# Sixteen-head attention: the step for the next operands moved in front of the weighing by key in VectorE's order

## The reference

```python
qkv = (x @ w_qkv.T + b_qkv).reshape(B, T, 3, H, dh)
std_logits = jnp.einsum('bhqd,bhkd->bhqk', q, k) * scale
write_lines = exterior(w1, w2)      # six numbers for each head and position, from x and the position before
read_lines = exterior(r1, r2)
incidence = jnp.einsum('bqhp,bkhp->bhqk', read_lines, J_write)
weights = decays[:, None, None] ** diffs_pos[None] * past[None]
bias = incidence * weights[None] * bias_scale[None, :, None, None]
logits = jnp.where(causal_mask, -jnp.inf, std_logits + bias)
attn = jax.nn.softmax(logits, axis=-1)
out = jnp.einsum('bhqk,bhkd->bqhd', attn, v).reshape(B, T, D)
return out @ w_out.T + b_out
```

## Time and profile before

| | |
|---|---|
| median of 3 runs | 1036.51 us (1032.13 to 1037.96) |
| the profiled execution | 1033.47 us, its span 1032.2 us |
| busy PE, DVE, ACT, POOL | 856.5, 742.6, 655.6, 405.4 us |
| TensorE's granted clock, mean | 0.944 of full |
| the loop over heads | from 328 us to about 838 us; one batch of slots takes 61.5 us |
| chain that ended last | PE 44%, DVE 11%, issue 5%, ACT 5% |

### The profile page before, as it was taken

The page is one execution under the profiler, slowest core; times in us unless marked ns, Lnnn a source line. Parts: engine busy times, 40 slices in busy tenths (PEclk is TensorE's granted clock), DMA queues, the critical chain, the costliest instruction groups (busy, mean ns, idle before and its releaser), DMA issues.

```text
span 1032.2 us, 25478 instructions
## 1 busy us (share of the span) xinstructions
PE 856.5 (83%) x9999; PEld 530.8 (51%) x9999; DVE 742.6 (72%) x1783; ACT 655.6 (64%) x1154; POOL 405.4 (39%) x664
## 2 busy tenths in 40 slices
PE   5688788876565698998989899898888868898987
PEld 2344455554433465665656566575565533444434
DVE  4776888898665868777686877868777557666554
ACT  4668888746234275766667575666656747685866
POOL 3043555455866535373543645454132210101000
PEclk8899999998866599999999999999999989999999
DMA  5000000000324252443525334262542000000000
GB/s 149 22 0 1 1 1 0 1 1 1 105 62 121 68 152 69 116 128 80 148 63 140 86 97 122 68 178 47 143 133 66 3 1 1 22 2 21 1 22 21
DMA packets 70698, 63.60 MB, mean 62 GB/s; under 512 B 30600, under 2 KB 62824, under 8 KB 70576
## 3 DMA queue, kind: packets, MB, share of 16 engines
q1 hardware_dynamic: 70064, 61.90, 22.7%
q10 hardware_dynamic: 512, 0.02, 0.0%
HBM read 34.02 MB, written 27.36 MB: 59 GB/s over the span
## 4 chain that ended last, share of the span: by engine, by line
PE 44%; DVE 11%; issue 5%; ACT 5%; POOL 1%; SPq 1%; DMA 1%; DVEq 0%; POOLq 0%; ACTq 0%
PE bank L2082 12%; PE bank L1660 7%; PE bank L1635 3%; PE bank L1608 3%; PE bank L1616 3%; PE bank L1597 2%; PE bank L1590 2%; DVE bank L1744 2%; PE bank L1600 2%; ACT 4g L2140 1%; PE bank L1668 1%; PE bank L1626 1%; DVE 4f L2176 1%; PE bank L1623 1%; DVE roots L1299 1%
## 5 line engine op out<-in xcount | busy, mean ns | idle before, releaser
L1824 ACT ACTIVATE ET<-bank 64x512 f32<-64x512 f32 x128 | 75.3, 589 | 100.3 <-PE bank L1626 99.5
L2163 DVE TENSOR_TENSOR act<-4f,act 128x512 f16<-128x512 f32 x96 | 66.4, 691 | 56.1 <-ACT act L2130 55.9
L1819 ACT ACTIVATE ET<-bank 128x768 f32<-128x768 f32 x128 | 103.1, 805 | 2.4
L1744 DVE TENSOR_TENSOR bank<-bank,W 128x256 f32<-128x256 f32 x128 | 54.7, 427 | 52.6 <-PE bank L1590 52.6
L1660 PE MATMUL bank<-ET,vv 128*32 128x128 f32 (+2 forms) x1792 | 90.0, 326 | 0.8 <-DVE O L1779 0.8
L1754 DVE TENSOR_REDUCE mo<-bank 128x4 f32<-128x512 f32 x128 | 87.3, 682 | 1.6 <-PE bank L1600 1.4
L1749 DVE TENSOR_TENSOR bank<-bank,WT 128x256 f32<-128x256 f32 x128 | 55.1, 430 | 46.1 <-PE bank L1616 43.2
L2130 ACT ACTIVATE act<-4f 128x512 f16<-128x512 f32 x96 | 60.4, 630 | 28.3 <-DVE 4f L2176 26.2
L1762 DVE TENSOR_REDUCE mo<-bank 128x3 f32<-128x384 f32 x128 | 70.0, 547 | 0.0
L1763 DVE TENSOR_REDUCE mo<-bank 128x3 f32<-128x384 f32 x128 | 69.9, 546 | 0.0
L2082 PE MATMUL bank<-act,std 128*128 128x512 f16 x256 | 57.0, 383 | 0.1
(11 more groups left out here) (376 smaller groups left out, 2542.1 us busy)
## 6 DMA issues: line engine op xcount, KB each, us to landing
ring<-scr_q SPq DMA_DIRECT2D x16, 324.0 KB
QO<-scr_q SPq DMA_DIRECT2D x16, 324.0 KB
ring<-scr_a SPq DMA_DIRECT2D x16, 252.0 KB
KA<-scr_a SPq DMA_DIRECT2D x16, 252.0 KB
ring<-scr_k SPq DMA_DIRECT2D x16, 168.0 KB
KB<-scr_k SPq DMA_DIRECT2D x16, 168.0 KB
scr_a<-dk SPq DMA_DIRECT2D x8, 288.0 KB, 2.6
X<-in_x SPq DMA_DIRECT2D x8, 256.0 KB, 5.2
```

Of the source, the lines that this page charges most:

```text
L1744: dve.tensor_tensor(half(psD, 1), half(psD, 1), over(W[:, h * HB:(h + 1) * HB], NT), ALU.mult).then_inc(s_wq, 1)
L1819: act.activation(ET[n % NE][:, T:SEG * P], psXT[:, 0:NP * P], ACT.Exp).then_inc(s_expo, 1)
L1824: act.activation(to[0:HB, :], psDT[0:HB, :], ACT.Exp)
L2163: dve.tensor_tensor(lo, f32_[f % 3], hi, ALU.subtract).then_inc(s_lo, 1)
```

## The change

One line moves in DVE's loop: `side(n)` goes from the end of the slot, behind `normalise` and `residual`, to between `largest_on_diagonal(n)` and `weigh_by_key(j)`. PE's, ACT's, POOL's and SP's orders stay as they are, and so does every instruction and every wait.

```diff
                 if n < HEADS:
                     largest_on_diagonal(n)
+                side(n)
                 if 0 <= j < HEADS:
                     weigh_by_key(j)
                 q = group_at(n, 4)
@@
                 b = rows_at(n, 1)
                 if b is not None:
                     residual(b)
-                side(n)
                 behind.dve(n)
```

## The result

| | before | after |
|---|---|---|
| median of runs, us | 1036.8 (1032.1 to 1039.2) | 1052.9 (1052.1 to 1057.5), 6 runs |
| ratio to before | | 1.0173, 95% interval [1.0143, 1.0202] |
| the profiled execution: time, span, us | 1033.5, 1032.2 | 1052.5, 1051.2 |
| its mean granted clock | 0.944 | 0.928 |

The kernel became slower by 16.1 us between the medians; the two profiled spans differ by 19.0. By the starts of L1744, 1.3 of these 19.0 lie in front of the loop, 1.3 in its slots 0 to 15, 14.3 in slots 16 to 111 and 2.1 behind them. The forecast was 1049, with 1041 to 1056 as the range.

The account below looks back on a forecast made before the run. PE was taken as nearly the bound, its standing still setting the time. 1033.47 + 10.6 for the order + 2.1 for three clock falls gave 1046.2, or 1049 on the median's level; range 1041 to 1056.

Parts of the forecast that it names:

- slot 2: Second slot of a batch: filling DVE's 0.43 us wait does not pay for 0.57, so PE's L1597 shifts by +0.14 us.
- slot 5: Slot where DVE's step waits for ACT's `raw`: L1749 now starts only when the step ends, L1597 +0.91 us.
- slot 6: Slot with a step 1.48 us long: L1597 at 473.42 instead of 472.37, of which +0.14 us is new.
- slot 7: Slot built like slot 5, with the step waiting for ACT: another +0.91 us, together +1.96.
- slot 8: Last slot with a step: gives 0.39 us back because `normalise` now lies beside PE's L1623 and L1635; shift +1.57.
- Slot 9: Slot following slot 8: ACT may hold PE's L1616, making the shift +1.64 us instead of +1.57.
- One stated sign of being wrong: Forecast is wrong if L1597 comes less than 1.4 us behind L1749 in the slots with a step.
- The sum: Loop's batches: 5 x (0.14 + 1.64) + (0.14 + 1.57) = 10.6 us, and nothing for batch 1.
- The clock: PE's stop of 2.43 us in slot 5 brings 0 to 6 clock falls, 0.7 us each; three taken, +2.1 us.
- A: Rival, L1749 to L1597: DVE is the bound, waits are filled, PE's queue does not pay; 1033 to 1037 us, chance 0.12.
- B: Rival: the clock falls in every batch with little cover, 10.6 + 10 us, giving 1057; chance 0.12.
- C: Rival: the 3.18 us DMA wait in front of slot 112 swallows the last batch's shift; 1.7 less, 1047; chance 0.08.

## Why the prediction was right

**The slots.** Set the starts of L1597 in the timeline after against those of the earlier trace rows, each from that of slot 2 (453.16 before, 458.79 after). PE's shift grows in slot 2 by 0.11 where 0.14 was predicted (L1597 of slot 3 stood at 457.46 before). In slot 5 it grows by 0.89 (468.48 became 475.11; predicted 0.91), in slot 6 by 0.13 (0.14), in slot 7 by 0.89 (0.91), in slot 8 by -0.40 (-0.39). Slot 9 adds 0.12, where ACT was given 0.07. The batch is 1.74 longer where 1.77 was said, 63.29 where 63.3 was said. From slot 10 to the end of the batch the shift stays, as predicted. One stated sign of being wrong is met by the letter: L1597 stands 1.36 behind L1749 in slot 5 (473.75 to 475.11), and "less than 1.4" was the sign. It was set too tight, since the prediction's own sum has 0.49 + 0.89 = 1.38 there.

**The sum.** At full clock four batches are longer by 1.74 each, the last by 1.6, and the first by 2.5, together 11.1; predicted were 10.6. The step that was mis-sized is slot 2 of the first batch. The prediction gave all of these slots +0.14, as if the step never waited there, and in slot 18 it waits for POOL: +0.88, the same as in slots 5 and 7 and for the same reason.

**The clock.** This is the other term that was mis-sized. The mechanism held, and so did the price of one fall: five falls cost 3.6 us, 0.7 each, as was taken. But there were five and not three. So the loop has 11.1 for the order and 3.6 for the clock, less 0.4 that the wait for DMA in front of slot 112 took up: 14.3, where 12.7 was predicted.

**Outside the loop.** The prediction has nothing there, and the profile has 4.7 us more: 1.3 in front of the loop, 1.3 in batch 1 and 2.1 behind slot 112. The 1.3 in batch 1 go with the clock's late rise, and the order of slot 8, the one thing that the change moves there, isn't needed for it. Why this one execution was later in the other two places stays open. The 16.1 between the medians don't tell how much of this an average execution has. The forecast of 1049 is good by its slots; that the median came within 4 us of it, with three falls taken of a possible six and nothing taken outside the loop, is in part luck.

**The rivals.** A, the waits are filled and PE doesn't pay: out. L1597 stands 0.89 behind L1623 in every pair, and the waits only changed place. B, a fall in every batch with little cover: the number was nearly right, five of six, but one cost 0.7 and not 1.7, since `values` lies beside DVE's step as argued. C, the DMA wait of slot 112 swallows the last batch's shift: it is 2.8 now and was 3.18, so 0.4 was swallowed, and the load moved with the slots for the rest.

The Trainium skill (TensorE: Matmul & The Clock Gate, Why this matters for your kernels) asks to keep PE's idle gaps under some 3 us. The falls in the loop after came behind stops of 2.34 us (four) and of 1.50 us (one), and none came in the slots where these stops were filled, so by this case's runs the bound is too generous.

## What to carry to other kernels

A step moved in front of an instruction takes its waits along, but everything that the other engine does behind that instruction now starts later: compare the wait that is filled (0.43 here at most) with the work that loses its cover (0.89 here, 0.57 when the hand-over times of the two orders are taken off), slot by slot. And look for waits that don't show: slot 18 cost 0.75 us more than its likes because another engine was done just in time. A wait inside a step is better filled with the step's own ready work than by moving the step; that gave 0.7% where the move cost 1.7%. And a long stop of TensorE can cost more than its length, since it can also bring the clock down: look at the longest wait, not only at the total.

## What was not expected of the hardware

- A stop of PE brought the clock down sometimes and not always, and the longest one most often. In slots 16 to 111 of all twelve profiles, without the wait for DMA in front of slot 112, the clock fell behind 12 of 15 stops of 2.34 us, 1 of 6 of 2.1 us, 2 of 5 of 1.9 us and 5 of 25 of 1.5 us. It fell behind none of the nine of 1.57 and none of those of 1.2 to 1.4, and no fall there lies elsewhere. Each fall lasted 3.5 to 4 us; the five in the kernel after cost 0.4 to 1.0 us, 0.7 in the mean.
- PE's doing 3.3 us more of useless work per batch made the kernel faster, ratio 1.0111 instead of 1.0173 to the kernel before; some of that lies outside the filled slots.
- The moment at which the clock rises in the first slots of the loop differs by 13 us between profiles (357 to 370), which is worth more than a microsecond, and no edit tried here set it. In a kernel of 1 ms with changes of some 5 us, one profile isn't enough to tell such a term; the loop at full clock is.
